# Shared-key attention: sums of a pair of items inverted as 128x32 instead of 128x512, values and sums interleaved

## The chip, the cores and the metric

One core of a Trainium2 chip runs the kernel. The time is the device time of one execution in microseconds (us). The kernel before takes 1633.4 us (median of 3 runs, 1633.3 to 1633.51).

## The reference, cut to what matters

The program is four blocks, each an attention and a feed-forward layer, each followed by a residual addition and a layer norm, over 2048 rows of 256. The change lies in the attention of the second block (L1), which has 16 query heads of 16 elements and one key and one value head for all of them:

```python
def _L1_attn_ref(x, Wq, Wk, Wv, Wo, bo):
    q = (x @ Wq).reshape(Bsz, Tlen, H, D)      # H = 16, D = 16, Tlen = 2048
    k = x @ Wk
    v = x @ Wv
    scores = jnp.einsum('bihd,bjd->bhij', q, k) / jnp.sqrt(jnp.float32(D))
    scores = jnp.where(causal, scores, -jnp.inf)
    attn = jax.nn.softmax(scores, axis=-1)
    out = jnp.einsum('bhij,bjd->bihd', attn, v).reshape(Bsz, Tlen, C)
    return out @ Wo + bo
```

## The kernel before, in words

The rows are cut into 4 chunks of 512 (`CH`), and the heads into 4 groups of 4. An **item** is a chunk with a group of heads, 16 in all (item i has chunk i // 4). For each item the kernel goes through **blocks** of 128 keys, 4, 8, 12 or 16 of them by the chunk; there are 160 blocks, and `P1.first[i]` is the first of item i (0, 4, 8, 12, 16, 24, 32, 40, 48, 60, 72, 84, 96, 112, 128, 144). All engines run through the same list of **steps** n, from -7 to 163, each with its own instructions of that step, in program order:

- TensorE computes the scores of block n + 1 into one of three banks (`score`, L1194; L1198 adds the mask), and the values of block n (`value`, L1208): 32 output rows per head, 16 of them the weighted values, 16 all equal to the sum of the exponentials (the columns of `VX` from 16 on hold ones). Between them it computes score tiles of a coming item for its row maxima (`unit`, L1163, L1166), into two pairs of banks in turn; a pair is used again only when VectorE has reduced it.
- ScalarE takes the exponentials (`exps`, L1275), four of 512 columns a block, and after an item's last block copies its values and sums into `OT` (`values_out`, L1281; `OT` holds four items).
- VectorE reduces each unit's tile to its maxima (L1345), joins the halves of them (L1349) and copies the turned maxima (L1368) for SyncE to place (`maxima_rows`, L999).
- SyncE issues all transfers of this layer, in program order (`l1_sp`).

Two items with the same chunk and neighbouring groups make a **pair** (8 pairs). When the first has been evacuated, `join` (L1009) moves its sums by 4 transfers into `D`; when the second has been, it moves that one's values beside the first's values in `OT`, and its sums into `D`, by 8 transfers (L1022, L1023). `D` and the joined half of `OT` are 128x512: 8 heads by 16 elements, each sum repeated 16 times. Then VectorE, for each quarter of 128 columns, inverts the sums (`inverse`, L1355) and multiplies (L1360), into `AN`. For pairs 0 to 6 these 8 instructions stand in four steps, 2 to 5 after the pair's last block (2, 2, 3, 3 for the first two pairs), among the units; for pair 7 they stand behind the loop. `out` (L1212, L1221) multiplies `AN` with `Wo` for chunks 0 to 2 in the steps from 140 on, and for chunk 3 behind the loop. Behind a chunk's `out` VectorE adds the residual (L201, which waits for `f_ready`), takes the layer norm's statistics and norms (L228).

The next layer's weights are loaded by `l1f_loads` (L1579, 8 transfers, L1588), which SyncE issues behind `join(14)`; its own wait is for `f_ready` of chunk 0. VectorE waits for all 8 in `hadamard_sums` at step 148 (L1623, L1624), and GpSimd in `fold_down` (L1644, L1645).

Of the kernel before, what the change touches and what calls it, by code (L numbers as in the profile page):

```python
# [825 lines left out]
ROWS_OF_HIGH, ROWS_OF_MID, ROWS_OF_LOW = (0, 3, 5), (1, 4), (2,)  # L826


INVERSE_FIRST1, INVERSE_AT1 = (2, 2, 3, 3), (2, 3, 4, 5)


class Plan1:


    def __init__(self):
        self.first = [0]
        self.blocks = []
        self.units = []
        self.last_unit = []
        for i in range(NI1):  # L840
            c, g = i // 4, i % 4
            for j in range(TPC * (c + 1)):
                self.blocks.append((i, j, P * max(0, j - TPC * c)))
            self.first.append(len(self.blocks))
            for t in range(TPC):
                n = P * (t + 1)
                for h in range(0, G1, 2):
                    if c == 0:
                        self.units.append((i, t, h, 2, 0, 1, n))
                    if c == 1:  # L850
                        self.units += [(i, t, h, 1, 0, 2, n), (i, t, h + 1, 1, 0, 2, n)]
                    if c == 2:
                        self.units += [(i, t, h, 1, 0, 2, CH), (i, t, h + 1, 1, 0, 2, CH), (i, t, h, 2, 2, 1, n)]
                    if c == 3:
                        self.units += [(i, t, h, 1, 0, 2, CH), (i, t, h, 1, 2, 2, n),
                                       (i, t, h + 1, 1, 0, 2, CH), (i, t, h + 1, 1, 2, 2, n)]
            self.last_unit.append(len(self.units) - 1)
        self.nb = len(self.blocks)
        self.steps = range(-AHEAD1, self.nb + 4)
        self.units_at, self.mt_at, self.join_at, self.inv_at, self.out_at, self.turn_at, self.sum_at = {}, {}, {}, {}, {}, {}, {}  # L860
        done = 0
        for n in self.steps:
            upto = self.units_by(n)
            self.units_at[n] = range(done, upto)
            done = upto
        for i in range(NI1):
            self.mt_at[self.first[i] - 4] = i
            c = i // 4
            self.join_at[self.first[i + 1]] = i
            if i % 2 == 1:  # L870
                for j in range(TPC):
                    self.inv_at.setdefault(self.first[i + 1] + (INVERSE_FIRST1 if c == 0 else INVERSE_AT1)[j], []).append((i // 2, j))
        for c in range(NC - 1):
            s = self.nb - 20 + 5 * c
            for j in range(TPC):
                self.out_at[s + j] = (c, j)
            self.sum_at[s + TPC] = c
            self.turn_at[s + TPC + 4] = c
        self.unit_ring, self.mt_ring = {}, {}
        a = 0  # L880
        for n in self.steps:
            if n in self.mt_at:
                self.mt_ring[self.mt_at[n]] = a
                a += 1
            for u in self.units_at[n]:
                self.unit_ring[u] = a
                a += 1
# [13 lines left out]

P1 = Plan1()
FIRST1, LAST1 = -AHEAD1, NC - 1
JOINS1 = 12
HIGHS1 = [(1, 2), (4, 5), (7, 7), (9, 9)]
VALUES1 = [3, 6, 8, 10]
RES1 = [2, 4, 5, 6]
# [5 lines left out]
def l1_alloc(k):  # L913
# [23 lines left out]
    a.r1 = v(normed + 6 * part, [P, 3, CH])  # L937
    a.OT = take([P, 4, CH])
    a.D = take([P, CH])
    a.w = take([P, KT, QKV1])  # L940
    a.wo = take([P, 2, E])
    a.bias = take([P, E])
# [10 lines left out]
    a.MT = take([P, 2, CH], BF16)  # L953
    assert o <= 41000, o
    s = k.sem
    a.joined = s("l1_heads_and_sums_joined")
    a.ld, a.ldo, a.z = s("l1_weights_loaded"), s("l1_wo_loaded"), s("l1_buffers_set")
    a.prj, a.ev = s("l1_projected"), s("l1_high_and_v_evacuated")
    a.res, a.mid, a.low = s("l1_residual"), s("l1_middle_part"), s("l1_low_part")
# [10 lines left out]
def l1_sp(k, sp, I):  # L970
# [29 lines left out]
                     a.MT[0:MROWS * G1, i % 2, :]).then_inc(a.mrow, 16)  # L1000

    sp.wait_ge(a.z, 1)
    wo = I["L1_attn_Wo"].rearrange("(g r d) e -> r d g e", r=4, d=D0)
    for r in range(4):
        low, high = slice(32 * r, 32 * r + D0), slice(32 * r + D0, 32 * r + 2 * D0)
        for dst, src in ((a.wo[low, :, :], wo[r][:, 0:4:2, :]), (a.wo[high, :, :], wo[r][:, 1:4:2, :])):
            sp.dma_start(dst, src).then_inc(a.ldo, 16)

    def join(i):  # L1009
        pair, even = i // 2, i % 2 == 0  # L1010
        sp.wait_ge(a.ot, i + 1)
        if even and pair >= 1:
            sp.wait_ge(a.joined, 16 * JOINS1 * pair)
            sp.wait_ge(a.an, TPC * pair)
        if not even:
            sp.wait_ge(a.joined, 16 * (JOINS1 * pair + 4))
        for r in range(4):
            low, high = slice(32 * r, 32 * r + D0), slice(32 * r + D0, 32 * r + 2 * D0)
            if even:
                sp.dma_start(a.D[low, :], a.OT[high, i % 4, :]).then_inc(a.joined, 16)  # L1020
            else:
                sp.dma_start(a.OT[high, (i - 1) % 4, :], a.OT[low, i % 4, :]).then_inc(a.joined, 16)  # L1022
                sp.dma_start(a.D[high, :], a.OT[high, i % 4, :]).then_inc(a.joined, 16)  # L1023

    stack_chunk(0)
    stack_chunk(1)
# [4 lines left out]
    for n in P1.steps:  # L1031
        if P1.mt_at.get(n, 0) >= 2:
            maxima_rows(P1.mt_at[n])
        if n in P1.join_at:
            join(P1.join_at[n])
            if P1.join_at[n] == NI1 - 2:
                l1f_loads(k, sp, I)


def l1_project(k, pe, c, half):  # L1040
# [35 lines left out]
def l1_high(k, act, c, half):  # L1076
# [6 lines left out]
    if c < 2 and half == 0:  # L1083
        return
    act.wait_ge(a.prj, VALUES1[c])
    act.activation(a.VX[:, TPC * c:TPC * (c + 1), 0:D0],
                   PS[:, first + (1 if c < 2 else 3), TPC * D0 * c:TPC * D0 * (c + 1)].rearrange("p (j d) -> p j d", d=D0),
                   ACT.Copy).then_inc(a.ev, 1)

# [37 lines left out]

def l1_set(k, pool, st):
    a = k.l1
    pool.memset(a.VX[:, :, D0:32], 1.0).then_inc(a.z, 1)  # L1130
    pool.wait_ge(a.ld, L1_LOADS)
    pool.tensor_copy(a.mqb, a.mq).then_inc(a.z, 1)
    pool.tensor_copy(a.mkb, a.mk).then_inc(a.z, 1)
# [5 lines left out]
def l1_pe(k, pe):  # L1139
# [72 lines left out]
    def out(c, j):  # L1212
        t = TPC * c + j
        if j == 0:
            pe.wait_ge(k.r_done, NC * 2 + c)
        pe.wait_ge(a.an, TPC * (2 * c + 1) + j + 1)
        if t == 0:
            pe.wait_ge(a.ldo, 16 * 8)
            pe.wait_ge(a.m1, P1.mt_ring[NI1 - 1] + 1)
        for g in range(2):  # L1220
            last = pe.matmul(f_tile(k, j, F1_BANK), a.AN[:, g, P * t:P * (t + 1)], a.wo[:, g, :], start=g == 0, stop=g == 1)  # L1221
# [40 lines left out]
def l1_act(k, act, st):  # L1262
# [14 lines left out]
    def values_out(i):  # L1277
        act.wait_ge(a.pv, P1.first[i + 1])
        if i >= 4:
            act.wait_ge(a.an, TPC * (i // 2 - 1))  # L1280
        act.activation(a.OT[:, i % 4, :], PS[:, 7, :], ACT.Copy).then_inc(a.ot, 1)  # L1281

    for n in P1.steps:
# [43 lines left out]
def l1_dve(k, dve, st):  # L1327
# [20 lines left out]
        dve.wait_ge(a.m1, P1.unit_ring[P1.last_unit[i]] + 1)  # L1348
        dve.tensor_tensor(a.NM[:, i % 2, :, :], a.MA[:, i % 2, 0, :, :], a.MA[:, i % 2, 1, :, :], ALU.min).then_inc(a.nm, 1)  # L1349

    def inverse(pair, j):
        cols = slice(P * j, P * (j + 1))
        if j == 0:
            dve.wait_ge(a.joined, 16 * JOINS1 * (pair + 1))
        st.link(dve.reciprocal(a.D[:, cols], a.D[:, cols]))  # L1355
        c = pair // 2
        if pair == 0 and j == 0:
            for par in range(2):
                dve.wait_ge(a.stack[par], 16 * SPLIT_DMAS * 2)
        dve.tensor_tensor(a.AN[:, pair % 2, CH * c + P * j:CH * c + P * (j + 1)], a.OT[:, 2 * (pair % 2), cols], a.D[:, cols],  # L1360
                          ALU.mult).then_inc(a.an, 1)

    def maxima_rows(i):
        x = P1.mt_ring[i]
# [6 lines left out]
    for n in P1.steps:  # L1371
# [6 lines left out]
        for u in P1.units_at[n]:  # L1378
            unit(u)
            if u in P1.last_unit and P1.units[u][0] >= 8:  # L1380
                combine(P1.units[u][0])
        if n in P1.inv_at and n < P1.nb:
            for pair, j in P1.inv_at[n]:
                inverse(pair, j)
        if n in HADAMARD_AT1:
            hadamard_sums(k, dve, st, HADAMARD_AT1[n])
        if n in P1.sum_at:
# [3 lines left out]
    for n in range(2):  # L1391
        hadamard_out(k, dve, n)
    for j in range(TPC):
        inverse(NI1 // 2 - 1, j)
    for n in range(2, 4):
        hadamard_out(k, dve, n)
    dve.wait_ge(a.biased, NC)
# [1854 lines left out]
```

## Time and profile before

| | us |
|---|---|
| median of 3 runs | 1633.4 |
| the profiled execution's own time | 1633.87 |
| its span, first to last instruction | 1632.1 |
| TensorE busy | 1532.2 (94%) |
| VectorE busy | 1061.0 (65%) |
| ScalarE busy | 780.0 (48%) |
| GpSimd busy | 359.6 (22%) |
| mean granted TensorE clock | 0.986 |

The shared-key attention takes the span from about 199 to 709 us. In the profile PE is TensorE, PEld its weight loads, DVE VectorE, ACT ScalarE, POOL GpSimd, SP SyncE and SPq the transfers that it issues. L12 is line 12 of the kernel. A busy share is an average over stages with different limits, so each stage is read by itself.

### The profile page before, as it was taken

How to read it: one execution, taken by the hardware profiler on the slowest of the kernel's cores; microseconds unless marked ns; L12 is line 12 of the kernel's file. 1: busy time of each engine (PE TensorE's matmuls, PEld its weight loads, DVE VectorE, ACT ScalarE, POOL GpSimd, SP SyncE). 2: the span in 40 equal slices, each digit the busy share in tenths (PEclk: the TensorE clock that was granted, in tenths of full speed). 3: DMA queues.
4: the chain of work that ended last, by engine and by line, in shares of the span. 5: the costliest groups of instructions: out<-in, count | busy, mean ns of one | idle time of the engine just before them, and what ended most of it. 6: DMA issues, size and time to landing. Idle time of an engine off the chain costs nothing.

```text
span 1632.1 us, 35751 instructions
## 1 busy us (share of the span) xinstructions
PE 1532.2 (94%) x14924; PEld 948.7 (58%) x14924; DVE 1061.0 (65%) x1913; ACT 780.0 (48%) x1793; POOL 359.6 (22%) x405
## 2 busy tenths in 40 slices
PE   7999988989989999799999979999999999999998
PEld 4666554444444444345557547777777777774556
DVE  4668789888898883543534885447777877942223
ACT  2431336767767877422111143357767767642110
POOL 2222010000010001400000024434545545640000
PEclk9999989999999999899999999999999999999999
DMA  6000230000000003010000031000000020000000
GB/s 190 2 2 7 78 84 20 13 8 11 9 6 10 6 10 113 7 53 0 17 0 0 1 94 36 0 7 8 2 1 8 1 88 1 2 1 0 13 13 26
DMA packets 31446, 38.78 MB, mean 24 GB/s; under 512 B 7219, under 2 KB 26230, under 8 KB 30774
## 3 DMA queue, kind: packets, MB, share of 16 engines
q1 hardware_dynamic: 31286, 36.50, 7.4%
q8 instruction: 118, 1.93, 0.5%
q14 instruction: 42, 0.34, 0.1%
HBM read 23.74 MB, written 2.10 MB: 16 GB/s over the span
## 4 chain that ended last, share of the span: by engine, by line
PE 78%; DVE 13%; issue 3%; ACT 3%; SPq 1%; DMA 0%; POOL 0%; POOLq 0%; ACTq 0%; DVEq 0%
PE PS L1427 7%; PE PS L1433 7%; PE PS L1456 7%; DVE arena L1345 6%; PE PS L2670 6%; PE PS L1208 6%; PE PS L1163 6%; PE PS L1194 5%; PE PS L2177 3%; PE PS L2657 3%; PE PS L2635 3%; PE PS L340 2%; PE PS L2500 2%; PE PS L2147 2%; PE PS L2516 2%
## 5 line engine op out<-in xcount | busy, mean ns | idle before, releaser
L1275 ACT ACTIVATE arena<-PS 128x512 f32<-128x512 f32 (+3 forms) x640 | 315.3, 534 | 155.2 <-PE PS L1198 67.1
L1345 DVE TENSOR_REDUCE arena<-PS 128x1 f32<-128x1024 f32 (+7 forms) x320 | 325.9, 1058 | 49.7 <-PE PS L1166 34.6
L1194 PE MATMUL PS<-arena 99*32 99x512 bf16 (+3 forms) x2560 | 212.0, 352 | 1.5 <-ACT arena L1275 1.0
L1163 PE MATMUL PS<-arena 96*32 96x512 bf16 (+3 forms) x2560 | 183.8, 355 | 28.3 <-DVE arena L1345 25.7
L1208 PE MATMUL PS<-arena 128*32 128x512 f32 (+3 forms) x1280 | 149.3, 540 | 2.4 <-ACT arena L1281 1.7
L191 POOL TENSOR_TENSOR rstd<-ve,mhalf 128x4 f32<-128x4 f32 x31 | 31.7, 1022 | 510.7 <-DVE ve L219 510.6
L1163 PEld LDWEIGHTS PS<-arena 96*32 96x32 bf16 x2560 | 62.0, 98 | 109.2 <-DVE arena L1345 58.9
L2821 ACT ACTIVATE arena<-arena 128x128 f32<-128x128 f32 x256 | 122.7, 484 | 0.0
L1427 PE MATMUL PS<-XT,arena 128*128 128x512 f32 x256 | 120.4, 592 | 0.9 <-DVE arena L1664 0.9
L2670 PE MATMUL PS<-arena 128*128 128x256 f32 x512 | 121.0, 379 | 0.2
L1433 PE MATMUL PS<-XT,arena 128*128 128x512 f32 x256 | 120.3, 592 | 0.0
L1456 PE MATMUL PS<-arena 128*128 128x256 f32 x512 | 112.8, 379 | 1.9 <-DVE R L201 1.9
L1194 PEld LDWEIGHTS PS<-arena 99*32 99x32 bf16 x2560 | 69.4, 97 | 75.4 <-ACT arena L1275 34.2
L1456 PEld LDWEIGHTS PS<-arena 128*128 128x128 f32 x512 | 96.8, 190 | 20.2 <-issue 7.2
L2670 PEld LDWEIGHTS PS<-arena 128*128 128x128 f32 x512 | 97.0, 190 | 14.3 <-issue 1.3
L186 ACT ACTIVATE XT<-PS 128x1024 f32<-128x1024 f32 x28 | 28.7, 1024 | 142.6 <-PE PS L179 142.6
L1310 POOL CAST arena<-arena 128x16 bf16<-128x16 f32 x16 | 3.1, 196 | 414.8 <-DVE arena L1349 279.2
L2919 POOL TENSOR_TENSOR arena<-arena 128x512 f32<-128x512 f32 x64 | 66.5, 1040 | 121.9 <-DVE arena L3033 121.9
L2913 POOL TENSOR_TENSOR arena<-arena,mhalf 128x4 f32<-128x4 f32 x64 | 79.1, 1237 | 28.7 <-DVE arena L3006 28.7
L201 DVE TENSOR_TENSOR R<-PS,X 128x1024 f32<-128x1024 f32 x20 | 24.4, 1220 | 93.2 <-PE PS L1456 77.1
L1433 PEld LDWEIGHTS PS<-XT,arena 128*128 128x128 f32 x256 | 48.6, 190 | 61.2 <-issue 55.5
L1427 PEld LDWEIGHTS PS<-XT,arena 128*128 128x128 f32 x256 | 48.4, 190 | 59.3 <-issue 57.9
(248 smaller groups left out, 2743.5 us busy)
## 6 DMA issues: line engine op xcount, KB each, us to landing
arena<-arena SPq DMA_DIRECT2D x55, 128.0 KB, 2.4
arena<-arena SPq DMA_DIRECT2D x96, 32.0 KB, 2.0
XT<-in_L_attn_xT SPq DMA_DIRECT2D x4, 512.0 KB, 8.2
X<-in_L_attn_x SPq DMA_DIRECT2D x4, 512.0 KB, 9.9
arena<-in_L_attn_out_w SPq DMA_DIRECT2D x1, 2048.0 KB, 8.0
out<-X SPq DMA_DIRECT2D x3, 512.0 KB, 2.9
arena<-in_dmask SPq DMA_DIRECT2D x1, 1024.0 KB, 5.7
arena<-in_L_ffn_W_up SPq DMA_DIRECT2D x1, 1024.0 KB, 5.2
```

Of the source, the lines that this page charges most:

```text
L1163: last = pe.matmul(flat[p, o:o + w], q[:, p], a.KS[0:SROWS, CH * kc:CH * kc + w], start=True, stop=kc < c)
L1194: last = pe.matmul(PS[p, b, lo:CH], keys[:, p], a.QS[0:rows, G1 * g + r, CH * c + lo:CH * (c + 1)], start=True, stop=j < TPC * c)
L1208: last = pe.matmul(PS[32 * r:32 * r + 32, 7, lo:CH], a.VX[:, j, :], a.PB[:, n % 3, r, lo:CH], start=j == 0, stop=j == TPC * (c + 1) - 1)
L1275: act.activation(a.PB[:, n % 3, r, lo:CH], PS[:, 4 + x % 3, lo:CH], ACT.Exp, scale=D0 ** -0.5).then_inc(a.e2, 1)
L1345: dve.tensor_reduce(dst, src, AX.X, ALU.max, negate=True).then_inc(a.m1, 1)
L1427: last = pe.matmul(PS[:, n % 2, :], a.gate[:, kt, P * it:P * (it + 1)], k.XT[:, kt, CH * c:CH * (c + 1)], start=kt == 0, stop=kt == KT - 1)
L1433: last = pe.matmul(PS[:, 2 + n % 2, :], a.up[:, kt, P * it:P * (it + 1)], k.XT[:, kt, CH * c:CH * (c + 1)], start=kt == 0, stop=kt == KT - 1)
L1456: last = pe.matmul(F, a.h[:, c % 2, it, P * j:P * (j + 1)], a.down[:, it, :], start=it == 0, stop=it == HT - 1)
L2670: last = pe.matmul(f_tile(k, t % TPC), a.AT[:, n % 4, i, :], a.W12[:, h, :], start=h == 0, stop=h == H - 1)
L2821: last = act.activation(a.Pr[:, n % 3, i, :], a.Pr[:, n % 3, i, :], ACT.Exp, bias=a.NM[:, t, h:h + 1], scale=a.rq[:, t, h:h + 1], accum_ou ...
L2913: pool.tensor_tensor(a.rq[:, t, hs], a.rq[:, t, hs], k.mhalf[:, 0:G3], ALU.pow).then_inc(a.q_rs, 1)
L2919: pool.tensor_tensor(p, p, bc(a.L[:, t, hs], 2, WK3), ALU.mult).then_inc(a.pn, 1)
```

## The change

The sum of a head now comes out in the odd one of each two output rows and the values in the even ones (`VX` and the rows of `Wo` are laid out to match; `Wo` is loaded by 2 transfers in place of 8). For pairs 0 to 6 one sum row per head (4 rows of 512) is spread over 64 partitions of 32 columns in `DC`, by one transfer per item; VectorE inverts 128x32 at step 2 after the pair's last block; one transfer brings the result back into 8 rows (`DR`, step 3); two transfers repeat each row 16 times into `D` (step 4); VectorE multiplies 128x512 in one instruction at step 7. Moving the second item's values beside the first's takes one transfer. Pair 7 keeps its four inversions and multiplications of 128 columns, with 3 transfers in place of 12, 2 of them after its second item. `l1f_loads` is issued ahead of `join(14)` rather than behind it. Counts in the waits follow (`an` counts pairs rather than quarters).

```diff
 ROWS_OF_HIGH, ROWS_OF_MID, ROWS_OF_LOW = (0, 3, 5), (1, 4), (2,)
 
 
-INVERSE_FIRST1, INVERSE_AT1 = (2, 2, 3, 3), (2, 3, 4, 5)
+PAIRS1, INVERSE1, ROWS1, SPREAD1, NORMED1 = 8, 2, 3, 4, 7
...
-            c = i // 4
             self.join_at[self.first[i + 1]] = i
-            if i % 2 == 1:
-                for j in range(TPC):
-                    self.inv_at.setdefault(self.first[i + 1] + (INVERSE_FIRST1 if c == 0 else INVERSE_AT1)[j], []).append((i // 2, j))
+            if i % 2 == 1 and i < NI1 - 1:
+                for at, table in ((INVERSE1, self.inv_at), (ROWS1, self.rows_at), (SPREAD1, self.spread_at), (NORMED1, self.norm_at)):
+                    table[self.first[i + 1] + at] = i // 2
...
-JOINS1 = 12
+MOVES1 = 16 * 6
...
+    a.DC = take([P, 32])
+    a.DR = take([P, CH])
...
-    a.joined = s("l1_heads_and_sums_joined")
+    a.moved, a.inv = s("l1_heads_and_sums_moved"), s("l1_sums_inverted")
...
-    wo = I["L1_attn_Wo"].rearrange("(g r d) e -> r d g e", r=4, d=D0)
-    for r in range(4):
-        low, high = slice(32 * r, 32 * r + D0), slice(32 * r + D0, 32 * r + 2 * D0)
-        for dst, src in ((a.wo[low, :, :], wo[r][:, 0:4:2, :]), (a.wo[high, :, :], wo[r][:, 1:4:2, :])):
-            sp.dma_start(dst, src).then_inc(a.ldo, 16)
+    wo = I["L1_attn_Wo"].rearrange("(g u m) e -> u m g e", u=2, m=H * D0 // 4)
+    for par in range(2):
+        sp.dma_start(a.wo[par:P:2, :, :], wo[par]).then_inc(a.ldo, 16)
 
     def join(i):
         pair, even = i // 2, i % 2 == 0
+        last = pair == PAIRS1 - 1
+        ot = lambda n, rows: a.OT[rows, n % 4, :]
+        values, sums, head_sums = slice(0, P, 2), slice(1, P, 2), slice(1, P, 32)
         sp.wait_ge(a.ot, i + 1)
-        if even and pair >= 1:
-            sp.wait_ge(a.joined, 16 * JOINS1 * pair)
-            sp.wait_ge(a.an, TPC * pair)
-        if not even:
-            sp.wait_ge(a.joined, 16 * (JOINS1 * pair + 4))
-        for r in range(4):
-            low, high = slice(32 * r, 32 * r + D0), slice(32 * r + D0, 32 * r + 2 * D0)
-            if even:
-                sp.dma_start(a.D[low, :], a.OT[high, i % 4, :]).then_inc(a.joined, 16)
+        if even:
+            if pair >= 1:
+                sp.wait_ge(a.moved, MOVES1 * pair)
+            if last:
+                sp.wait_ge(a.an, pair)
+                sp.dma_start(a.D[values, :], ot(i, sums)).then_inc(a.moved, 16)
             else:
-                sp.dma_start(a.OT[high, (i - 1) % 4, :], a.OT[low, i % 4, :]).then_inc(a.joined, 16)
-                sp.dma_start(a.D[high, :], a.OT[high, i % 4, :]).then_inc(a.joined, 16)
+                sp.dma_start(a.DC[0:P // 2, :], ot(i, head_sums)).then_inc(a.moved, 16)
+        else:
+            sp.wait_ge(a.moved, MOVES1 * pair + 16)
+            if last:
+                sp.dma_start(a.D[sums, :], ot(i, sums)).then_inc(a.moved, 16)
+            else:
+                sp.dma_start(a.DC[P // 2:P, :], ot(i, head_sums)).then_inc(a.moved, 16)
+            sp.dma_start(ot(i - 1, sums), ot(i, values)).then_inc(a.moved, 16)
+
+    def inverse_rows(pair):
+        sp.wait_ge(a.inv, pair + 1)
+        sp.dma_start(a.DR[0:2 * G1, :], a.DC).then_inc(a.moved, 16)
+
+    def spread(pair):
+        sp.wait_ge(a.moved, MOVES1 * pair + 16 * 4)
+        if pair >= 1:
+            sp.wait_ge(a.an, pair)
+        for par in range(2):
+            sp.dma_start(a.D[par:P:2, :], bc(a.DR[G1 * par:G1 * (par + 1), :], 1, D0)).then_inc(a.moved, 16)
 
     stack_chunk(0)
     stack_chunk(1)
     for n in P1.steps:
         if P1.mt_at.get(n, 0) >= 2:
             maxima_rows(P1.mt_at[n])
+        if n in P1.rows_at:
+            inverse_rows(P1.rows_at[n])
+        if n in P1.spread_at:
+            spread(P1.spread_at[n])
         if n in P1.join_at:
-            join(P1.join_at[n])
             if P1.join_at[n] == NI1 - 2:
                 l1f_loads(k, sp, I)
+            join(P1.join_at[n])
...
-    act.activation(a.VX[:, TPC * c:TPC * (c + 1), 0:D0],
+    act.activation(a.VX[:, TPC * c:TPC * (c + 1), 0:2 * D0:2],
...
-    pool.memset(a.VX[:, :, D0:32], 1.0).then_inc(a.z, 1)
+    pool.memset(a.VX[:, :, 1:2 * D0:2], 1.0).then_inc(a.z, 1)
...
-        pe.wait_ge(a.an, TPC * (2 * c + 1) + j + 1)
+        pe.wait_ge(a.an, 2 * c + 2 if c < NC - 1 else PAIRS1 + j)
         if t == 0:
-            pe.wait_ge(a.ldo, 16 * 8)
+            pe.wait_ge(a.ldo, 16 * 2)
...
-            act.wait_ge(a.an, TPC * (i // 2 - 1))
+            act.wait_ge(a.an, i // 2 - 1)
...
-    def inverse(pair, j):
-        cols = slice(P * j, P * (j + 1))
-        if j == 0:
-            dve.wait_ge(a.joined, 16 * JOINS1 * (pair + 1))
-        st.link(dve.reciprocal(a.D[:, cols], a.D[:, cols]))
+    def inverse(pair):
+        dve.wait_ge(a.moved, MOVES1 * pair + 16 * 3)
+        dve.reciprocal(a.DC, a.DC).then_inc(a.inv, 1)
+
+    def normed(pair):
         c = pair // 2
-        if pair == 0 and j == 0:
+        if pair == 0:
             for par in range(2):
                 dve.wait_ge(a.stack[par], 16 * SPLIT_DMAS * 2)
-        dve.tensor_tensor(a.AN[:, pair % 2, CH * c + P * j:CH * c + P * (j + 1)], a.OT[:, 2 * (pair % 2), cols], a.D[:, cols],
-                          ALU.mult).then_inc(a.an, 1)
+        dve.wait_ge(a.moved, MOVES1 * (pair + 1))
+        dve.tensor_tensor(a.AN[:, pair % 2, CH * c:CH * (c + 1)], a.OT[:, 2 * (pair % 2), :], a.D, ALU.mult).then_inc(a.an, 1)
+
+    def last_normed(j):
+        pair, cols = PAIRS1 - 1, slice(P * j, P * (j + 1))
+        if j == 0:
+            dve.wait_ge(a.moved, MOVES1 * pair + 16 * 3)
+        st.link(dve.reciprocal(a.D[:, cols], a.D[:, cols]))
+        dve.tensor_tensor(a.AN[:, pair % 2, CH * LAST1 + P * j:CH * LAST1 + P * (j + 1)], a.OT[:, 2 * (pair % 2), cols],
+                          a.D[:, cols], ALU.mult).then_inc(a.an, 1)
 
     def maxima_rows(i):
         x = P1.mt_ring[i]
             unit(u)
             if u in P1.last_unit and P1.units[u][0] >= 8:
                 combine(P1.units[u][0])
-        if n in P1.inv_at and n < P1.nb:
-            for pair, j in P1.inv_at[n]:
-                inverse(pair, j)
+        if n in P1.inv_at:
+            inverse(P1.inv_at[n])
+        if n in P1.norm_at:
+            normed(P1.norm_at[n])
...
-        inverse(NI1 // 2 - 1, j)
+        last_normed(j)
```

## Rows read from the trace of the kernel before

**Rows 1.** The page: chain that ended last; one group (busy, mean | idle before, releaser).
```profile
PE 78%; DVE 13%; issue 3%; ACT 3%; SPq 1%; DMA 0%; POOL 0%; POOLq 0%; ACTq 0%; DVEq 0%
...
L1163 PEld LDWEIGHTS PS<-arena 96*32 96x32 bf16 x2560 | 62.0, 98 | 109.2 <-DVE arena L1345 58.9
```

**Rows 2.** Windows, L1281 to L1281: length; busy PE, PEld, DVE, ACT, POOL; clock; DMA, GB/s.
```profile
258.05:270.87 12.82, 11.30 (x260) 6.33 (x264) 11.85 (x17) 7.12 (x19) 0.00 (x0) 0.87 0.06 14
270.87:293.32 22.45, 20.09 (x460) 10.28 (x456) 20.19 (x26) 15.79 (x34) 0.84 (x4) 1.00 0.06 15
293.32:313.51 20.19, 19.73 (x460) 10.43 (x456) 15.97 (x18) 15.67 (x35) 0.84 (x4) 1.00 0.04 10
313.51:341.87 28.36, 23.79 (x504) 10.89 (x496) 26.89 (x32) 15.96 (x34) 0.84 (x4) 1.00 0.05 12
...
364.37:398.51 34.14, 31.10 (x616) 14.36 (x612) 29.99 (x35) 24.83 (x51) 3.31 (x5) 1.00 0.04 10
398.51:429.85 31.34, 30.54 (x616) 14.81 (x612) 25.75 (x27) 24.42 (x50) 3.18 (x5) 1.00 0.03 7
429.85:467.25 37.40, 33.42 (x652) 15.16 (x648) 34.52 (x39) 24.78 (x50) 3.29 (x5) 1.00 0.04 10
...
502.03:545.82 43.79, 41.35 (x776) 18.62 (x772) 39.29 (x43) 33.48 (x67) 0.83 (x4) 1.00 0.04 9
545.82:587.00 41.18, 40.72 (x776) 19.00 (x772) 35.03 (x35) 33.10 (x66) 0.84 (x4) 1.00 0.03 6
```

**Rows 3.** Groups of VectorE's instructions by shape (count | busy, mean ns).
```profile
L1355 DVE RECIPROCAL arena<-arena 128x128 f32<-128x128 f32 x32 | 30.2, 943 | 4.0 <-DMA arena<-arena 4.0
...
L3033 DVE RECIPROCAL arena<-arena 128x4 f32<-128x4 f32 x64 | 11.4, 178 | 2.2
...
L1360 DVE TENSOR_TENSOR arena<-arena 128x128 f32<-128x128 f32 x32 | 9.3, 292 | 1.1
...
L1919 DVE TENSOR_TENSOR arena<-arena 128x512 f32<-128x512 f32 x8 | 5.5, 693 | 0.3
```

**Rows 4.** The page's DMA issues (count, KB each, us to landing).
```profile
arena<-arena SPq DMA_DIRECT2D x55, 128.0 KB, 2.4
arena<-arena SPq DMA_DIRECT2D x96, 32.0 KB, 2.0
```

**Rows 5.** SyncE's issue for the coming item's maxima, in the sixth item.
```profile
304.79 0.77 SPq L999 DMA_DIRECT2D arena<-arena  x1
```

**Rows 6.** DMA view of 577 to 581 us, where that issue (12 KB) alone lands.
```profile
DMA packets 16, 0.02 MB, mean 5 GB/s; under 512 B 3, under 2 KB 15, under 8 KB 15
```

**Rows 7.** Chain that ended last, 625 to 710 us (start, us, what).
```profile
634.31 0.59 SPq L1588
...
637.28 12.62 issue
```

**Rows 8.** TensorE's waits, 640 to 720 us (in total, times, longest).
```profile
PE PS L1221 <- DVE R L201: 6.8, 1, 6.8
```

**Rows 9.** VectorE's first L201 of this layer, in order of time.
```profile
631.47 1.22 DVE L201 TENSOR_TENSOR R<-PS,X 128x1024 f32<-128x1024 f32 x1 [10.05 <-PE PS L1221]
```

**Rows 10.** Instructions of all engines in order of time, 683 to 699 us.
```profile
684.22 0.52 SPq L1022 DMA_DIRECT2D arena<-arena  x1
684.79 0.59 SPq L1023 DMA_DIRECT2D arena<-arena  x1
...
690.60 0.95 DVE L1355 RECIPROCAL arena<-arena 128x128 f32<-128x128 f32 x1 [4.05 <-DMA arena<-arena]
...
692.03 6.33 PE L1221 MATMUL PS<-arena 128*128 128x256 f32 x16 [4.55 <-DVE arena L1360]
...
698.47 1.23 DVE L201 TENSOR_TENSOR R<-PS,X 128x1024 f32<-128x1024 f32 x1 [1.70 <-PE PS L1221]
```

**Rows 11.** Busy time in the two stretches at half clock (columns as in rows 2).
```profile
653.02:663.26 10.24, 5.47 (x28) 1.99 (x28) 7.08 (x12) 1.32 (x3) 10.08 (x8) 0.50 0.00 0
690.56:697.39 6.83, 5.36 (x13) 4.26 (x14) 6.03 (x10) 0.00 (x0) 0.00 (x0) 0.50 0.00 0
```

More of the change, by code:

```diff
@@ L859, in __init__ @@
         self.steps = range(-AHEAD1, self.nb + 4)
-        self.units_at, self.mt_at, self.join_at, self.inv_at, self.out_at, self.turn_at, self.sum_at = {}, {}, {}, {}, {}, {}, {}
+        self.units_at, self.mt_at, self.join_at, self.inv_at, self.rows_at, self.spread_at, self.norm_at, self.out_at, self.turn_at, self.sum_at = \
+            {}, {}, {}, {}, {}, {}, {}, {}, {}, {}
         done = 0
```

## The prediction

> **What bounds the kernel now.** I read the page's chain of work that ended last first: TensorE holds 78% of the span, VectorE 13% [rows 1]. In the shared-key attention VectorE's 13% are not beside TensorE but in turn with it: TensorE's weight loads for the score tiles stood idle 58.9 us until a reduction (L1345) had freed a pair of banks [rows 1]. So here the question is when a VectorE instruction delays a reduction. The view that answers it is the busy time by window, cut at the evacuation of each item (L1281) [rows 2]. The reader should compare windows with the same blocks. The 9th item holds the four inversions of pair 3, the 10th has the same blocks and tiles and none: 34.14 and 31.34 us. The 13th (pair 5) and the 14th: 43.79 and 41.18. The 5th (pair 1) and the 6th: 22.45 and 20.19. Where there are no inversions TensorE is busy nearly throughout (40.72 of 41.18), and where there are, it is not. Last I read two places outside these windows: the chain around 637 us, where the next layer's loads hold everything up [rows 7], and the end of the layer, where pair 7's transfers do [rows 10].
>
> **1. VectorE's work for pairs 0 to 6.** Removed per pair: 4 inversions of 943 ns and 4 multiplications of 292 ns = 4.94 us [rows 3]. Added: one inversion of 128x32. No row has that shape; between 178 ns for 4 columns and 943 ns for 128 a column costs 765/124 = 6.2 ns, so 178 + 28 x 6.2 = 0.35 us. And one multiplication of 128x512, 0.69 us (L1919 has the shape and both inputs in the same memory) [rows 3]. VectorE has 4.94 - 1.04 = 3.90 us less a pair, 27.3 in all. That is the upper bound; what it is worth at the end is less, since VectorE had slack that absorbed part of the old work.
> Pair by pair, from rows 2:
> - Pair 3: 34.14 - 31.34 = 2.80. Pair 5: 43.79 - 41.18 = 2.61. Pair 6 sits in the 15th item, with the same first eleven blocks as the 13th; I take 2.6 too. Pair 1: 22.45 - 20.19 = 2.26.
> - Pair 2: its item (28.36 us) also reduces the tiles of the first item of chunk 2, three a step, and VectorE is busy 26.89 of it. There nearly every microsecond off VectorE counts: from 2.3 (as pair 1) to 3.9 (all); 28.36 can't go below TensorE's 23.79. I take 3.6, near the end of the range that a 95% busy engine is nearest to.
> - Pair 4: the item is 37.40 with VectorE busy 34.52. The inversions come ahead of its crowded steps, as in pair 3 (2.80), but the new multiplication at step 7 falls within them and costs its full 0.69, while some backlog that used to be carried goes: I take 2.3, bounds 2.1 and 3.9.
> - Pair 0: 12.82 us with VectorE busy 11.85 and a clock of 0.87, so VectorE bounds it; bounds 2.3 and 3.9, I take 2.8.
> The sum is 2.8 + 2.3 + 3.6 + 2.8 + 2.3 + 2.6 + 2.6 = 19.0. Against it stands the new work in the windows of pairs 3, 5 and 6. It is split into 0.35 and 0.69, five steps apart, and the 10th item shows VectorE idle 31.34 - 25.75 = 5.6 us, so it mostly fits; I charge 0.2 each. **18.4 us**, from 13 (if backlog hides half more than these pairs show) to 23.
>
> **2. The chain that the new work waits for.** VectorE's multiplication now stands in program order in front of reductions and waits for the two repeating transfers; these wait for the transfer back, and that for the inversion. SyncE issues them in its one order behind the maxima transfer (L999) of the same step. The shortest cover is in pairs 0 and 1, whose steps 4 to 7 are short diagonal blocks. The 6th item shows the same place without inversions: L999 starts at 304.79 and takes 0.77 [rows 5], the item ends at 313.51 [rows 2]. Two issues of 0.6 each (the spacing of rows 10) put the second at 306.2; a transfer of 128 KB lands after 2.4 us [rows 4], at 308.6. Cover left: 4.9 us. In chunks 1 to 3 three steps of full blocks are longer. So the wait costs nothing. What is queued on SyncE behind each new wait is the next `join`, which has steps to spare. The first inversion waits for 3 transfers where it waited for 12: no later than now.
> These two transfers read 4 rows each, and the trace has one with few rows: the 12 KB of L999 left 12 data packets and 3 short ones in its window [rows 6], so a transfer with 12 and 3 rows seems to have run on 3 engines. The Trainium skill (DMA: Bandwidth & Descriptors, Why a DMA increments its semaphore by 16 and not by 1) says that the number of engines is the largest up to 16 that divides the slowest dimension of both sides. By this rule each repeating transfer runs on 4 engines rather than 16, each with four times the share. The trace agrees as far as those 3 short packets go. From rows: 128 KB in 2.4 us against 32 KB in 2.0 [rows 4] is 0.4 us for 96 KB over 16 engines, so 4 engines and 256 KB need some 0.4 x (256/96) x 4 = 4.3 us on top of 2: landing at about 311.9 rather than 308.6, with 1.6 us of cover left. Still hidden, but barely: that is a rival below.
>
> **3. The next layer's loads.** Their first issue starts at 634.31, behind the four of `join(14)`; VectorE's L1623, which waits for all eight, starts at 649.90, and the chain runs through that wait [rows 7]. TensorE then stands 6.8 us waiting for L201, behind L1623 and L1624 on VectorE [rows 8]. In the changed order the loads wait for chunk 0's `out` alone; that was done when L201 started, at 631.47 [rows 9]. They go out 634.31 - 631.47 = 2.84 us sooner, everything up to L201 comes as much sooner, and TensorE's wait of 6.8 shrinks to 4.0 and can give all of it: **2.8 us**. `join(14)` now stands behind eight issues, some 7.6 us; its sums aren't needed before 684 us, so that costs nothing. Bounds: 0 (if the loads' landing were set by something else) and 2.8.
> After the wait TensorE ran at half clock until 663.26, 5.47 us of work [rows 11], of which full clock would give back up to 2.7. With 4.0 us of standing the grant probably still falls but is back sooner: **0.7 us**, bounds 0 and 2.7.
>
> **4. The end of the layer.** The eight transfers of pair 7 were issued from 684.22 on, one each 0.63 us, and the last landed at 690.60, when VectorE had waited 4.05 us [rows 10]. Two remain, issued at 684.22 and 684.79; with 2.4 us for 128 KB the second lands at 687.2: 3.4 us sooner. VectorE is free from 690.60 - 4.05 = 686.55, before that. TensorE's wait of 4.55 us becomes 1.1, so the half clock of 690.56 to 697.39 [rows 11] should go too. L1221's 16 matmuls took 6.33 us [rows 10]; at full clock VectorE's pace of 943 + 292 ns = 1.2 per quarter [rows 3] sets it, 3 x 1.2 and a last group of 1.1 = 4.7: 1.6 sooner. **5.0 us** in all, bounds 3.0 (the half clock stays) and 5.3.
>
> **5. Costed at nothing.** Six transfers fewer for `Wo`: they are issued ahead of SyncE's wait for chunk 0's projections, which covers either number. The strided copy and fill of `VX` have the same element counts. Matmul shapes don't change.
>
> **The sum.** 18.4 + 2.8 + 0.7 + 5.0 = 26.9. Behind 709 us the stages start from the end of this layer, so the shift is carried to the end. The profiled execution took 1633.87, giving 1607.0; the median of the runs is 0.47 lower, 1633.4, giving **1606.5**.
>
> **The rivals.**
> - *The slack takes it* (8%): TensorE, 78% of the chain, becomes the bound at once, and only a third of part 1 comes through, 6 us: saved 14.5, time 1618.9. Against it speak the windows with and without inversions, which measure just that difference.
> - *The repeating transfers come late* (7%): by 4 engines and busy queues, VectorE waits 1 to 2 us in pairs 0 and 1 and some tenths elsewhere: costs 3 to 5 us, time 1610.5. This is what the rule on engines would decide, if its 4.3 us were 6.
> - *VectorE stalls in order, slower* (3%): the chain of issue, landing, inversion, landing, repeat, landing is so long that the multiplication waits in all 7 pairs, with the reductions behind it. From the point where each wait passes 26.9/7 = 3.8 us the kernel loses; at 5 us it is 35 - 26.9 = 8 slower, 1641.5. It needs landings of over 10 us; small transfers between rows took 2.0 to 2.4 [rows 4].
> - *The loads gain nothing and the clock stays* (5%): 1611.
>
> **Chances.** The forecast has 77%, with its own range 1602 to 1611 from the bounds of parts 1, 3 and 4. For 8 in 10 I reach to the late transfers and part of the slack rival: 1601.5 to 1613. About 0.2% (3.3 us) is what a measurement here can tell from none. Faster by more: 0.95; within: 0.02; slower by more: 0.03.
>
> **What would show it.** In the profile after, the windows from L1281 to L1281 of the 9th, 13th and 5th items should come within 0.3 us of the 10th, 14th and 6th. One inversion of 0.35 us per pair, no idle time of VectorE before the 128x512 multiplication (more than 0.3 us there speaks for the late transfers). The first load's issue right after chunk 0's `out`, 2.8 us before its old place relative to L201, and TensorE's wait for the second L201 near 4 us. Pair 7's first inversion about 3 us after its evacuation's end. If the 10th and 14th items themselves change, or VectorE's idle time moves without the windows shrinking, part 1 is wrong.

## The result and the profile after

The changed kernel takes 1614.45 us (median of 4 runs, 1613.19 to 1615.96), the kernel before 1633.35 beside it: ratio 0.9884, 95% interval 0.9869 to 0.9899. It is 18.9 us faster where 26.9 were forecast, and lies 1.5 us above the range. The profiled execution took 1613.19, its span is 1611.4.

Busy time by window, cut at the item evacuations as in [rows 2] (the line is now L1302); the windows are the 4th to 7th, the 9th to 11th and the 13th item:

```profile
256.75:265.88 9.13, 9.02 (x248) 5.43 (x252) 7.64 (x10) 6.99 (x19) 0.00 (x0) 1.00 0.18 25
265.88:291.22 25.34, 21.43 (x460) 10.56 (x456) 16.77 (x20) 15.76 (x34) 0.84 (x4) 0.93 0.12 20
291.22:314.20 22.98, 19.93 (x460) 10.25 (x456) 16.57 (x19) 15.79 (x35) 0.83 (x4) 1.00 0.04 7
314.20:339.25 25.05, 23.43 (x504) 10.89 (x496) 22.91 (x25) 15.86 (x34) 0.83 (x4) 1.00 0.12 20
...
361.94:393.28 31.34, 30.54 (x616) 14.82 (x612) 26.55 (x29) 24.42 (x51) 3.17 (x5) 1.00 0.10 17
393.28:424.62 31.34, 30.54 (x616) 14.80 (x612) 25.76 (x27) 24.42 (x51) 3.17 (x5) 1.00 0.01 3
424.62:459.49 34.87, 32.95 (x652) 15.47 (x648) 31.04 (x33) 24.47 (x50) 3.17 (x5) 1.00 0.09 15
...
494.26:536.06 41.80, 40.89 (x776) 18.87 (x772) 35.86 (x37) 33.15 (x66) 0.84 (x4) 1.00 0.08 13
```

The 9th item now takes what the 10th does, 31.34 us, as it should. But the 5th grew from 22.45 to 25.34 although its inversions are gone, and the 6th, which never had any, from 20.19 to 22.98. VectorE's work does not explain it: it is busy 16.77 us in the 5th (20.19 before) and 16.57 in the 6th (15.97 before). Its groups by shape, and its waits from 255 to 300 us, say why:

```profile
L1382 DVE TENSOR_TENSOR arena<-arena 128x512 f32<-128x512 f32 x7 | 4.8, 689 | 7.9 <-DMA arena<-arena 7.9
L1388 DVE RECIPROCAL arena<-arena 128x128 f32<-128x128 f32 x4 | 3.8, 948 | 0.5 <-DMA arena<-arena 0.5
L1374 DVE RECIPROCAL arena<-arena 128x32 f32<-128x32 f32 x7 | 2.4, 342 | 0.0
```

```profile
DVE arena L1382 <- DMA arena<-arena: 7.1, 2, 4.0
```

The new multiplication (L1382) waited 7.9 us for transfers, 7.1 of them in pairs 0 and 1. The chain that ended last shows the wait on the path (255 to 275 us):

```profile
254.99 0.27 DVE arena L1374
...
255.27 3.46 DMA arena<-arena
...
258.75 0.64 SPq L1040
...
259.44 10.74 DMA arena<-arena
...
270.30 0.69 DVE arena L1382
```

The second repeating transfer (L1040) lands 10.7 us after its issue, where the prediction had 2.4. Its other price, 2 + 4.3 = 6.3 us by the rule on engines, was for both transfers and counted from the first one's issue; from there it took 11.4 us (258.75 to 270.18). The prediction held both prices to be hidden.

It helps to cut the span at three places that every kernel here has: **A** from the second evacuation to the 15th (all of pairs 0 to 6), **B** from there to the 16th (the next layer's loads), **C** from there to the end (pair 7's transfers and all behind). The start of the program is left out: in the profile of before TensorE ran at half clock (1.2 of 2.4 GHz) from 123.95 us for 3.4 us and in this one it did not (0.79 and 1.00 granted over 122 to 130 us). This puts the events behind it 1.6 us apart, 1.3 of which is left at the second evacuation, and has nothing to do with the change. The forecast's 18.4 is part 1, with nothing for the wait of part 2; its 3.5 is part 3 with the clock, its 5.0 part 4.

| us | span | A | B | C |
|---|---|---|---|---|
| before | 1632.1 | 386.40 | 52.43 | 948.47 |
| changed | 1611.4 | 375.94 | 48.49 | 943.50 |
| gain | 20.7 | 10.5 | 3.9 | 5.0 |
| forecast | | 18.4 | 3.5 | 5.0 |
| multiplication of pairs 0, 1 two steps later | 1604.6 | 368.26 | 49.22 | 943.52 |
| rows 4 apart | 1605.2 | 366.96 | 49.83 | 943.57 |
| eight repeating transfers | 1606.3 | 368.68 | 49.14 | 943.48 |
| loads behind the join | 1611.4 | 373.46 | 51.21 | 943.38 |
| rows 16 apart | 1605.2 | 366.93 | 49.89 | 943.45 |
| rows 4 apart, pair 7 in eight transfers | 1607.3 | 366.87 | 48.66 | 948.47 |
| rows 4 apart, pair 4's multiplication later | 1602.4 | 366.29 | 49.32 | 943.50 |
| the same, first load alone | 1600.0 | 366.38 | 44.79 | 943.11 |

All of the shortfall is in A.

Below, the time of a block is that from its first exponential on ScalarE to the next block's.

### The profile page after: what moved, and what is told of

It reads as the page before. It is cut to its first block, busy times and chain, and to the rows that moved or that the text cites. A ratio compares the mean times of both kernels' runs of the same rounds, so it can differ in the third digit from the quotient of the medians.

```text
span 1611.4 us, 35658 instructions
## 1 busy us (share of the span) xinstructions
PE 1527.3 (95%) x14924; PEld 945.3 (59%) x14924; DVE 1037.1 (64%) x1871; ACT 778.4 (48%) x1793; POOL 357.9 (22%) x405
## 4 chain that ended last, share of the span: by engine, by line
PE 78%; DVE 11%; DMA 4%; issue 3%; ACT 3%; SPq 1%; POOL 0%; POOLq 0%; ACTq 0%; DVEq 0%
PE PS L1457 7%; PE PS L1463 7%; PE PS L1486 7%; PE PS L2700 6%; PE PS L1229 6%; PE PS L1184 6%; PE PS L1215 5%; DVE arena L1366 4%; PE PS L2207 4%; PE PS L2687 3%; DMA arena<-arena 3%; PE PS L2665 3%; PE PS L340 2%; PE PS L2530 2%; PE PS L2177 2%
## 5 line engine op out<-in xcount | busy, mean ns | idle before, releaser
L191 POOL TENSOR_TENSOR rstd<-ve,mhalf 128x4 f32<-128x4 f32 x31 | 31.7, 1022 | 504.4 <-DVE ve L219 504.3
L201 DVE TENSOR_TENSOR R<-PS,X 128x1024 f32<-128x1024 f32 x20 | 24.4, 1220 | 91.5 <-PE PS L1486 77.1
```

## The experiments

**1. The multiplication later.** Theory: the wait for the transfers, in VectorE's program order, holds everything.

```diff
-                    table[self.first[i + 1] + at] = i // 2
+                    table[self.first[i + 1] + (9 if table is self.norm_at and i < 4 else at)] = i // 2
```

> The changed kernel with one edit: for pairs 0 and 1 the 128x512 multiplication stands at step 9 after the pair's last block instead of step 7 (the others keep 7). Theory A (the repeating transfers land too late, and VectorE, which waits for them in program order, holds the reductions and so TensorE): VectorE waited 4.0 us before pair 0's multiplication; two steps are 5.4 us, so its wait goes to 0, block 18 (7.88 us) falls to 2.7 and block 26 (5.51) to 2.7, and the span falls by 8 us to about 1603.5. Rival B (the 5.17 and 2.79 us lost in blocks 18 and 26 are the multiplication's own and its position's, not the wait's): they reappear two blocks later, and the span stays within 1 us of 1611.4.

The span is 1604.6, 6.8 us less where 8 were expected, and A is 7.7 us shorter than in the changed kernel; the median of 4 runs is 1606.43, ratio to before 0.9837 (0.982 to 0.9853). VectorE in order of time shows the multiplication right behind a reduction, with no wait, at 272.31:

```profile
271.17 1.23 DVE L1366 TENSOR_REDUCE arena<-PS 128x1 f32<-128x1024 f32 x1 [0.36 <-PE PS L1187]
272.31 0.68 DVE L1382 TENSOR_TENSOR arena<-arena 128x512 f32<-128x512 f32 x1
272.91 1.61 DVE L1366 TENSOR_REDUCE arena<-PS 128x1 f32<-128x640 f32 x2
```

Blocks 18 and 26 fell from 7.88 and 5.51 to 2.7 us. What they lost does not reappear: block 20 grew by 0.45, and blocks 151 and 152 in B by 0.7. Theory A holds: the same transfers, as slow as before (the data of pair 0's two took 9.8 us in both), cost almost nothing once two more steps lie over them. 0.8 us of waiting is left, in pairs 5 and 6, which kept step 7.

**2. Why the transfers are slow: the rows' places.** Now the source is changed and the steps are left alone.

```diff
-        sp.dma_start(a.DR[0:2 * G1, :], a.DC).then_inc(a.moved, 16)
+        sp.dma_start(a.DR[0:32:4, :], a.DC).then_inc(a.moved, 16)
...
-            sp.dma_start(a.D[par:P:2, :], bc(a.DR[G1 * par:G1 * (par + 1), :], 1, D0)).then_inc(a.moved, 16)
+            sp.dma_start(a.D[par:P:2, :], bc(a.DR[16 * par:16 * par + 16:4, :], 1, D0)).then_inc(a.moved, 16)
```

> The changed kernel with the 8 rows of DR in partitions 0, 4, ..., 28 instead of 0 to 7; nothing else. In the changed kernel the packets of 2 KB of the repeating transfers took 309 ns in the middle (64 per transfer on 4 engines, 16 each, 5.2 us of data per transfer), where the same packets of other transfers between rows take 84. Theory P (the four engines read four neighbouring rows and get in each other's way at the source): the packets fall to 84 to 110 ns, a transfer's data to 1.3 to 1.8 us, both land some 7 us sooner, VectorE's wait in pairs 0 and 1 vanishes and the span falls by 8 us. Rival Q (the packets are slow since few engines with many packets each are slow): nothing changes, 309 ns and 1611.4 us.

The median packet fell from 309 ns to 84. Busy time over just the stretch in which pair 0's two transfers move their 256 KB (last column GB/s), first the changed kernel, then this one:

```profile
260.03:269.88 9.85, 8.47 (x204) 4.42 (x200) 5.91 (x7) 7.67 (x18) 0.00 (x0) 1.00 0.23 30
```

```profile
260.65:263.63 2.98, 2.98 (x104) 2.05 (x96) 2.59 (x3) 2.09 (x7) 0.00 (x0) 1.00 0.27 93
```

9.85 us of data against 2.98. VectorE waits for no transfer at any of the seven multiplications, and A is 366.96, 9.0 shorter than in the changed kernel. The span, 1605.2, is only 6.2 shorter, since B is 1.3 longer and TensorE had half clock from 13.8 us for 3.4 us, which put off the rest by 1.4. Theory P holds, Q falls. The windows of the 5th and 6th item are now equal, the comparison on which part 1 rested:

```profile
267.30:287.48 20.18, 19.72 (x460) 10.45 (x456) 16.68 (x20) 15.67 (x35) 0.83 (x4) 1.00 0.08 24
287.48:307.66 20.18, 19.72 (x460) 10.45 (x456) 16.57 (x19) 15.67 (x35) 0.84 (x4) 1.00 0.02 4
```

**3. Sixteen engines on one row.**

```diff
-MOVES1 = 16 * 6
+MOVES1 = 16 * 12
...
-            sp.dma_start(a.D[par:P:2, :], bc(a.DR[G1 * par:G1 * (par + 1), :], 1, D0)).then_inc(a.moved, 16)
+            for r in range(G1):
+                sp.dma_start(a.D[32 * r + par:32 * r + 32:2, :], bc(a.DR[G1 * par + r:G1 * par + r + 1, :], 1, D0)).then_inc(a.moved, 16)
```

> The changed kernel with the repetition by 8 transfers of one row to 16 rows each instead of 2 of 4 rows to 64. If the number of engines follows the slowest dimension, each now runs on 16 engines with one packet each. Theory Q: a transfer's data takes under 0.4 us, the last is issued 7 x 0.63 = 4.4 us after the first and lands 2.0 us later, 6.5 us after the first issue instead of 11: VectorE's wait in pair 0 falls from 4.0 us to under 0.5 and the span by 7 us. Theory P with sixteen engines reading one row: packets of over 1 us (16 at one row), each transfer's data over 1.2 us but still beside the next issue, so that the last lands about 8 us after the first issue: the wait falls to about 1 us, the span by 6.

Theory P again: the engines' share of busy time rises from 0.23 to 0.78 while the 256 KB still take 7.74 us; the median packet took 886 ns. More engines at the same rows bring the data from 9.85 us to 7.74, where theory Q had under 0.4 us for each of the eight transfers:

```profile
260.72:268.46 7.74, 7.18 (x205) 4.45 (x200) 6.73 (x7) 6.20 (x16) 0.00 (x0) 1.00 0.78 36
```

The wait before pair 0's multiplication is 1.08 us and A 368.68.

**4. The loads behind the join again**, in the changed kernel.

```diff
+            join(P1.join_at[n])
             if P1.join_at[n] == NI1 - 2:
                 l1f_loads(k, sp, I)
-            join(P1.join_at[n])
```

> The changed kernel with the next layer's loads issued behind join(14) again, as before the change. Theory A (the prediction's part 3): join(14) is one transfer now, so the loads are issued later by its wait for the evacuation and its issue, 0.4 + 0.6 = 1.0 us, and TensorE's wait for the second residual grows by 1.0 us: the span grows by about 1.0 us. Rival (what was gained at block 151, 3.8 us, is from the order): the span grows by 2.8 us or more.

TensorE's wait for the second residual is 5.1 us where it was 3.8: 1.3 more, near the 1.0 of theory A. B grew by 2.7; but the half clock behind the wait lasted 6.8 us here and 3.4 in the changed kernel. Experiments 1, 2, 3 and 5 have the loads ahead and 6.8 us of half clock too, and B is 49.14 to 49.89 in them, so that this order costs 1.3 to 2.1 us beside them. The span did not grow at all (1611.4), since A came out 2.5 shorter, for which the edit gives no reason.

That second thing is worth reading, first the changed kernel, then this one:

```profile
255.27 0.67 SPq L1033 DMA_DIRECT2D arena<-arena  x1
258.75 1.25 SPq L1040 DMA_DIRECT2D arena<-arena  x2
270.30 0.69 DVE L1382 TENSOR_TENSOR arena<-arena 128x512 f32<-128x512 f32 x1 [3.96 <-DMA arena<-arena]
```

```profile
255.14 0.68 SPq L1033 DMA_DIRECT2D arena<-arena  x1
257.83 1.22 SPq L1040 DMA_DIRECT2D arena<-arena  x2
269.26 0.69 DVE L1382 TENSOR_TENSOR arena<-arena 128x512 f32<-128x512 f32 x1 [3.07 <-DMA arena<-arena]
```

In the changed kernel's execution the transfer back (L1033) landed late, so that the repeating ones were issued 3.48 us behind it instead of 2.69, and pair 0's multiplication waited 0.9 us longer. Block 18 lost 5.17 us there and 2.75 here. There half clock followed the wait, from 271.90 to 275.31, and here none did. So of the 5.17 some 1.5 are left for the clock; no run tried this by itself. The same program text in A thus lost 9.0 us to the wait in one execution and 6.5 (373.46 - 366.96) in another.

**5. Which rows are apart.**

```diff
-        sp.dma_start(a.DR[0:2 * G1, :], a.DC).then_inc(a.moved, 16)
+        sp.dma_start(a.DR[0:P:16, :], a.DC).then_inc(a.moved, 16)
...
-            sp.dma_start(a.D[par:P:2, :], bc(a.DR[G1 * par:G1 * (par + 1), :], 1, D0)).then_inc(a.moved, 16)
+            sp.dma_start(a.D[par:P:2, :], bc(a.DR[64 * par:64 * par + 64:16, :], 1, D0)).then_inc(a.moved, 16)
```

> The changed kernel with the 8 rows of DR in partitions 0, 16, ..., 112. With rows 4 apart the packets of 2 KB fell from 309 to 84 ns; here is asked what 'apart' means. Theory (the port map of the Trainium skill, SBUF - State Buffer, Door 1: partitions 32 apart are on the same port): rows 0 and 32 share one, and 16 and 48, so two engines read at a port and packets take twice the free time, 150 to 170 ns, a transfer's data 2.5 us. Rival (only neighbouring rows meet): 84 ns, as with 4 apart. By both, the second transfer lands before VectorE asks for it, and the span is within 1 us of that with rows 4 apart, 1605.2.

The median packet took 156 ns, and the same 256 KB 4.70 us:

```profile
260.69:265.39 4.70, 4.70 (x156) 3.12 (x152) 4.31 (x5) 3.23 (x11) 0.00 (x0) 1.00 0.24 59
```

Rows 16 apart are worse than rows 4 apart: 4.70 us is about half of the 9.85 us of four neighbouring rows, as the theory has it where two of the four rows share a port, that is, one way into the memory. The rival of neighbourhood alone falls. The span is 1605.2, as both said.

**6. The loads ahead, alone**, in the kernel before.

```diff
-            join(P1.join_at[n])
             if P1.join_at[n] == NI1 - 2:
                 l1f_loads(k, sp, I)
+            join(P1.join_at[n])
```

> The kernel before with one edit: the next layer's loads are issued ahead of join(14) instead of behind it. Theory A (part 3 of the prediction): the first issue comes 2.8 us sooner and TensorE's wait for the second residual falls from 6.8 to 4.0 us; with 0 to 2.7 us of half clock given back the span falls by 2.8 to 5.5 us, to between 1626.6 and 1629.3. Rival (the gain at this place in the changed kernel needs the fewer transfers or the shorter join): less than 1 us.

The span is 1628.5, 3.6 us less; blocks 151 and 152 became 3.4 us shorter, and TensorE's wait fell from 6.8 to 4.4, by 2.4 where 2.8 were expected:

```profile
PE PS L1221 <- DVE R L201: 4.4, 1, 4.4
```

The half clock behind the wait lasted 3.4 us here and 10.2 before. Part 3 (3.5 us) holds by itself. A is 385.77 here and 386.40 in the kernel before: the latter had half clock in block 13, from 260.49 for 3.4 us, and this one had none.

**7. Pair 7's transfers in eight again**, on the kernel of experiment 2.

```diff
-                sp.dma_start(a.D[sums, :], ot(i, sums)).then_inc(a.moved, 16)
+                for r in range(4):
+                    ev, od = slice(32 * r, 32 * r + 32, 2), slice(32 * r + 1, 32 * r + 32, 2)
+                    sp.dma_start(ot(i - 1, od), ot(i, ev)).then_inc(a.moved, 16)
+                    sp.dma_start(a.D[od, :], ot(i, od)).then_inc(a.moved, 16)
```

> The kernel with rows 4 apart, and pair 7's last two transfers of 64 rows each cut back into eight of 16 rows, as before the change. Theory A (part 4): the last is issued 7 x 0.63 = 4.4 us after the first instead of 0.6 and lands 3.4 us later; TensorE's wait grows to 4.5 us, half clock comes back over the 16 matmuls with Wo, and everything behind the evacuation of the 16th item ends 5.0 us later: span 1610.2. Rival (the merged transfers of 128 KB land later than small ones and the clock is set by something else): under 2.5 us.

C is 948.47, as in the kernel before, 4.9 more than with two transfers. (That it agrees to the hundredth is chance: experiment 6, with the same eight transfers, has 948.16.) The span of 1607.3 is lower than the forecast 1610.2, since this execution had no half clock at 14 us, as experiment 2's had, and less of it in B; the comparison is C. The wait and the pace of the 16 matmuls, first here, then in the changed kernel:

```profile
665.75 0.95 DVE L1391 RECIPROCAL arena<-arena 128x128 f32<-128x128 f32 x1 [3.96 <-DMA arena<-arena]
...
667.18 6.10 PE L1245 MATMUL PS<-arena 128*128 128x256 f32 x16 [4.46 <-DVE arena L1392]
```

```profile
671.36 0.95 DVE L1388 RECIPROCAL arena<-arena 128x128 f32<-128x128 f32 x1 [0.52 <-DMA arena<-arena]
...
672.79 4.61 PE L1242 MATMUL PS<-arena 128*128 128x256 f32 x16 [1.02 <-DVE arena L1389]
```

**8. Pair 4's multiplication at step 11**, on the kernel of experiment 2.

```diff
-                    table[self.first[i + 1] + at] = i // 2
+                    table[self.first[i + 1] + (11 if table is self.norm_at and i == 9 else at)] = i // 2
```

> The kernel with rows 4 apart, and pair 4's multiplication at step 11 instead of 7. At step 7 it cost block 81 0.59 us, since it stood among VectorE's crowded steps; in the step 4 later VectorE has 1.5 us to spare, so those 0.6 us come back: span 1604.6, median about 1607, 1.65% faster than the kernel before and about 0.5% than the changed one. Rival (the multiplication costs its 0.69 us wherever it stands): 1605.2.

A fell from 366.96 to 366.29: block 81 has its 0.6 us back, and no other block of A changed by over 0.1. Median of 5 runs 1604.19, ratio to before 0.9825 (0.9812 to 0.9839). The rival falls. The span is 1602.4, 2.8 less; 1.6 of that lies ahead of A, where experiment 2's execution had the half clock at 14 us and this one had not.

**9. The first load alone**, on the kernel of experiment 8: the load of `W_up` gets its own semaphore, and the sum that reads only it waits for nothing else.

```diff
+    sp.dma_start(a.raw[:, 0, :, :], r(I["L1_ffn_W_up"])).then_inc(a.ld_up, 16)
...
-    if m == 0:
-        dve.wait_ge(a.ld, 16 * 8)
+    dve.wait_ge(*((a.ld_up, 16) if m == 0 else (a.ld, 16 * 7)))
```

> The best kernel so far (rows 4 apart, pair 4's multiplication at step 11), and VectorE's first sum of the next layer's weights (step 148) waits for the one load that it reads, on a semaphore of its own, instead of for all eight; the second sum, GpSimd and the first transform on TensorE still wait for the rest. What stands at blocks 151 and 152 is then seen whole. Theory A (VectorE stands 9.6 us in program order before the residual that TensorE waits for; that load lands 4.8 us after its issue): TensorE's remaining wait of 3.7 us goes, and with it the half clock behind it: block 151 falls from 8.7 us to about 4.5, the span by 4 to 6 us, to 1597 to 1598.5, and the median to about 1599. Rival (GpSimd's folding, which still starts when all have landed and shares VectorE's memory port, or the weights' landing, then holds the same place): under 2 us.

TensorE's wait for that residual is gone, and block 151 fell to 3.2 us. B is 4.5 shorter. The edit did more than move a wait: the two sums (L1653 and L1654 in the changed kernel), which took 3.4 us each beside GpSimd's folding, took 1.2 each here, where they ran ahead of it. How much of the gain is due to that no run tells apart. But block 154 grew by 1.8 us: the norm behind now waits for GpSimd, whose small operation (L191) stands behind its folding, and that still starts only when all loads have landed:

```profile
640.21 3.01 DVE L228 TENSOR_SCALAR X<-R,mv,rstd 128x256 f32<-128x256 f32 x4 [9.86 <-POOL rstd L191]
```

Both theories had a part. Median of 5 runs 1600.8, ratio to before 0.9804 (0.979 to 0.9817): the fastest kernel of this study. Its span of 1600.0 is above the forecast; up to the second evacuation this execution lost 2.4 us to experiment 8's, with half clock at 124.79 us for 3.4 us and a stretch of 23.9 us at 199.88 where that one had 20.5. The median is 3.4 us below experiment 8's and not the 5 of the forecast.

## Why the prediction was wrong

- **Part 1, VectorE's work, was right.** The inversion of 128x32 took 342 ns (0.35 forecast) and the multiplication 692 (0.69). Where the transfers land in time, A gains 386.40 - 366.96 = 19.4 us against 18.4; 0.6 of it is the half clock in block 13 of the kernel before. By pair, block by block in the changed kernel: pair 0 3.7 before its wait (2.8 forecast), pair 1 2.3 (2.3), pair 2 3.1 (3.6), pair 3 2.8, pair 4 2.5 (2.3), pairs 5 and 6 2.6 each. The multiplication at step 7 cost 0.6 in pair 4, as charged. The three charges of 0.2 were 0.1 or less each once it did not wait.
- **Part 2, "so the wait costs nothing", is the step that failed.** Its price was zero and it measured 9.0 us (375.94 - 366.96; 6.5 in experiment 4's execution): 5.2 in block 18 and 2.8 in block 26, and two times 0.5 in pairs 5 and 6, although three full blocks lie over the transfers there. The cover was forecast rightly: the second transfer's issue was to come 7.3 us ahead of VectorE's turn, and VectorE stood ready 6.9 us after it (266.34). The time to landing was wrong. I had taken the number of engines rightly: the transfers of 64 packets had 4 short ones each in the trace. I then priced four engines by scaling the difference between 32 KB and 128 KB [rows 4], which gave 4.3 us on top of 2, and held 6.3 us to be hidden. It was 11.4. Four engines were not the trouble: with the rows 4 apart the same four moved the data in 2.98 us, less than the 4.3. What the scaling could not see is where the packets read. The Trainium skill (SBUF — State Buffer, Door 1: The DMA port swizzle) says that partitions 0 to 3 share one port and that one port gives about 27 GB/s; by it the two transfers' 256 KB, each reading four rows behind one port, need an estimated 9.7 us. The trace agrees: 9.85 us from rows 0 to 7, 2.98 with the rows on ports of their own, 4.70 with two rows on each.
- **The rival "late" had the right consequence and place, the wrong cause and the wrong size**: it put the lateness down to four engines and busy queues, at 3 to 5 us and 7%. Its lateness of 1 to 2 us was 4.0 and 3.1. The last rival's 1611 does not come out of its terms: 2.8 + 0.7 lost give 1610.0.
- **Part 3 was right**: the first load's issue starts at 619.63, with L201 at 619.70, where before it came 634.31 - 631.47 = 2.84 us behind; TensorE's wait 3.8 (4.0), and 3.6 to 4.3 in the other executions of this order; with the clock 3.9 against 3.5, and 3.4 alone in experiment 6.
- **Part 4 was right**: 5.0 forecast, 4.97 measured, and undone by experiment 7. The wait before the 16 matmuls fell to 1.02 us (1.1), their time to 4.61 (4.7).
- **The range** of 1601.5 to 1613 holds the 1606.43 of experiment 1 and the 1604.19 of experiment 8, where pairs 0 and 1 do not wait. (Experiment 9, at 1600.8, changes more.) Its upper end reached out to the late transfers, but at a price of 3 to 5 us where they cost up to 9.0.

## What to carry to other kernels

A transfer that is moved off the path has to be priced by where it reads and writes, not only by its size: how many engines carry it, and how many memory ports its few source rows lie on. Repeating a handful of neighbouring rows was the slowest of the three placements tried here, and spacing the rows out cost nothing. When work that an in-order engine did is replaced by a round of transfers, the wait returns on that engine in front of unrelated work, so put the consumer some steps later, as far as its own readers allow, in a step where the engine has slack.

## What the runs showed of the hardware

- The same 256 KB, in packets of 2 KB on 4 engines: 9.85 us from rows 0 to 7, 4.70 from rows 16 apart, 2.98 from rows 4 apart; packets of 309, 156 and 84 ns. That they were 4 engines is read off the 4 short packets of each transfer. With 16 engines on one row after another 7.74 us, 34 GB/s, somewhat above the 27 that four engines had on rows 0 to 7. The first 64 packets, rows 0 to 3, were done after 4.8 us (27 GB/s) and the other 64 faster; why is open.
- Two VectorE sums of 128x1024 took 3.4 us each beside GpSimd's folding (changed kernel) and 1.2 each ahead of it (experiment 9).
- TensorE's half clock at about 124 us came in some executions and not in others of the same program part (in the profile of before and in experiment 9, not in the changed kernel's), worth 1.6 us there. Experiments 2, 3, 5 and 6 had such a stretch at about 14 us instead. Behind the loads' wait it lasted 3.4 or 6.8 us. Whether this makes the spread of 2.8 us between the four executions of the changed kernel is not shown, since one of them has a trace.
- So the span of a single execution can't settle a difference of 2 us here. The stretches between fixed events are steadier, each in its way: with the same program text C varies by 0.2 us, A by 0.1 where nothing waits, B by 1.4 with its half clock, and A by 2.5 where VectorE waits for late transfers.
